# Content products of a lambda layer: four neighbouring blocks of q read innermost, PSUM written in strides

## The reference

```python
def lambda_layer(x, ...):                      # B=32, 128 channels, 64 x 64 pixels, 4 heads, DIM_K=16, 32 values
    q = bn(conv1x1(x, q_w), ...)
    k = conv1x1(x, k_w)
    v = bn(conv1x1(x, v_w), ...)
    pos = position_lambdas(emb, v)             # a 15 x 15 convolution of every value plane, 16 kernels
    k = jax.nn.softmax(k, axis=1)
    ...
    content_lambda = jnp.einsum('bkm,bvm->bkv', k, v2)
    content_out = jnp.einsum('bhkn,bkv->bhvn', q, content_lambda)
    position_out = jnp.einsum('bhkn,bkvn->bhvn', q, pos)
    out = content_out + position_out
...
residual = x                                   # x is the group-normalised input, 512 channels
h = jax.nn.relu(bn(conv1x1(x, conv1_w), ...))
h = lambda_layer(h, ...)
h = jax.nn.relu(bn(h, ...))
h = bn(conv1x1(h, conv3_w), ...)
out = input + jax.nn.relu(h + residual)
```

## Time and profile before

| | |
|---|---|
| time, median of 3 runs | 5148.84 us (5134.06 to 5149.53) |
| profiled execution, its time | 5146.99 us |
| profiled execution, its span | 5145.2 us |
| mean granted TensorE clock | 0.935 of full speed |
| TensorE busy | 4617.9 us (90%) |
| VectorE, ScalarE, GpSimd busy | 2959.7, 2286.6, 747.9 us |
| content products (L603), busy | 246.1 us |

### The profile page before, as it was taken

The page is one execution under the profiler, slowest core; times in us unless marked ns, Lnnn a source line. Parts: engine busy times, 40 slices in busy tenths (PEclk is TensorE's granted clock), DMA queues, the critical chain, the costliest instruction groups (busy, mean ns, idle before and its releaser), DMA issues.

```text
span 5145.2 us, 120758 instructions
## 1 busy us (share of the span) xinstructions
PE 4617.9 (90%) x49366; PEld 2712.5 (53%) x49366; DVE 2959.7 (58%) x4695; ACT 2286.6 (44%) x2816; POOL 747.9 (15%) x433
## 2 busy tenths in 40 slices
PE   4888999888999988999999999999989999999997
PEld 2555555554555554555555555555555555555554
DVE  4466565565555565655655556556556555566564
ACT  1444445444444444444444444444444444444443
POOL 0011111111110111111111101111011111111111
PEclk8899999999999999999889999999999999999998
DMA  3778767778777787777786777877777877778766
GB/s 95 222 251 292 256 223 262 249 260 294 239 232 257 252 283 261 223 257 248 259 290 216 247 250 255 293 252 225 257 259 263 289 220 243 255 255 295 257 219 231
DMA packets 537174, 1284.17 MB, mean 250 GB/s; under 512 B 43048, under 2 KB 225324, under 8 KB 528556
## 3 DMA queue, kind: packets, MB, share of 16 engines
q1 hardware_dynamic: 471276, 1017.22, 60.4%
q10 hardware_dynamic: 65472, 260.05, 13.7%
HBM read 844.79 MB, written 432.33 MB: 248 GB/s over the span
## 4 chain that ended last, share of the span: by engine, by line
PE 49%; issue 14%; DMA 12%; DVE 8%; SPq 7%; POOL 5%; ACT 4%; ACTq 0%; POOLq 0%; DVEq 0%
PE ring L523 16%; DMA X<-x_dram 10%; PE ring L649 10%; PE ring L504 9%; POOL X L1175 5%; PE ring L579 4%; PE ring L530 3%; PE ring L603 2%; DVE st L871 2%; PE ring L535 2%; SPq L400 2%; SPq L358 2%; PE ring L613 2%; DMA q_parts<-region 1%; ACT region L789 1%
## 5 line engine op out<-in xcount | busy, mean ns | idle before, releaser
L698 ACT COPY region<-ring 126x1024 f32<-126x1024 f32 x1184 | 1164.1, 1016 | 1101.3 <-PE ring L504 1092.0
L579 PE MATMUL ring<-h,w3T 128*128 128x512 f32 x2048 | 1009.6, 636 | 105.7 <-DVE S L1018 73.6
L504 PE MATMUL ring<-Qt,Ep 96*126 96x256 bf16 x5120 | 832.8, 302 | 177.1 <-DVE region L698 80.4
L523 PE MATMUL ring<-X,w1e 128*128 128x512 f32 x2048 | 908.0, 596 | 29.3 <-DVE w1e L895 29.3
L649 PE MATMUL ring<-region,V 126*32 126x128 f32 x24576 | 866.7, 285 | 26.6 <-issue 26.2
L504 PEld LDWEIGHTS ring<-Qt,Ep 96*126 96x126 bf16 x5120 | 605.2, 148 | 420.2 <-issue 167.8
L649 PEld LDWEIGHTS ring<-region,V 126*32 126x32 f32 x24576 | 668.6, 114 | 245.5 <-issue 237.6
L698 DVE COPY region<-ring 126x1024 f32<-126x1024 f32 x352 | 430.2, 1222 | 616.1 <-PE ring L504 616.1
L871 DVE BATCH_NORM_STATS2 st<-X 128x6 f32<-128x512 f32 x1024 | 624.5, 678 | 212.1 <-DMA X<-x_dram 212.1
L579 PEld LDWEIGHTS ring<-h,w3T 128*128 128x128 f32 x2048 | 387.7, 201 | 534.9 <-issue 388.4
L523 PEld LDWEIGHTS ring<-X,w1e 128*128 128x128 f32 x2048 | 385.0, 191 | 496.9 <-issue 493.6
(11 more groups left out here) (127 smaller groups left out, 2960.3 us busy)
## 6 DMA issues: line engine op xcount, KB each, us to landing
X<-x_dram SPq DMA_DIRECT2D x132, 2048.0 KB, 20.2
out_dram<-X SPq DMA_DIRECT2D x512, 512.0 KB, 9.6
X<-x_dram ACTq DMA_DIRECT2D x124, 2048.0 KB, 10.5
Qt<-q_parts SPq DMA_DIRECT2D x768, 128.0 KB, 2.8
V<-v_windows SPq DMA_DIRECT2D x96, 1024.0 KB, 9.4
lambda_sums<-S SPq DMA_DIRECT2D x64, 1024.0 KB, 4.1
h<-lambda_sums SPq DMA_DIRECT2D x256, 256.0 KB, 4.9
q_parts<-region SPq DMA_DIRECT2D x128, 256.0 KB, 3.3
```

What stands on the lines that cost most here:

```text
L504: last = nc.tensor.matmul(dst[0:TROWS, i * 256:(i + 1) * 256], taps(u, xo, yo), Q[:, :, xo * BLK + yo, :], start=(i % 2 == 0), stop=True, ...
L523: last = nc.tensor.matmul(dst[:, hh * HALF:(hh + 1) * HALF], w1e[:, c, :], X[:, j, c, hh * HALF:(hh + 1) * HALF], start=(c == 0), stop=(c ...
L579: last = nc.tensor.matmul(dst[:, yb * HALF:(yb + 1) * HALF], w3T[:, t, :], src, start=True, stop=True)
L698: return engine_copy(dst, src)
```

## The change

The content products read q in the order head, pixel, block, which is the order of memory, so that runs of four blocks come together. The PSUM operand is given the same order of indices: the block, which was the outermost of its three indices and lies 128 elements apart, is now the innermost. Each element of q goes to the PSUM element it went to before. Number, size and order of the instructions stay.

```diff
                     for c in range(NCH):
-                        nc.tensor.matmul(bank_of(k)[c * DV:(c + 1) * DV, :], CLp[:, :],
-                                         Qg[:, :, c, half * 32:half * 32 + 32, 4 * k:4 * k + 4]
-                                         .rearrange("p h n b -> p b h n"),
+                        nc.tensor.matmul(bank_of(k)[c * DV:(c + 1) * DV, :]
+                                         .rearrange("p (b h n) -> p h n b", b=4, h=HEADS), CLp[:, :],
+                                         Qg[:, :, c, half * 32:half * 32 + 32, 4 * k:4 * k + 4],
                                          start=True, stop=False, skip_group_check=True)
```

## The result

| | before | changed |
|---|---|---|
| median of 4 runs each | 5148.74 us (5134.06 to 5149.53) | 5093.17 us (5086.59 to 5105.84) |
| ratio, 95% interval | | 0.9904 (0.9887 to 0.992) |
| profiled execution | 5146.99 us | 5105.84 us |
| mean granted clock in it | 0.935 | 0.924 |

The kernel is 1.0% faster, 56 us. The profiled execution of the changed kernel is the longest of its four; its span is 41.1 us shorter than that of before, so what the traces add up to is 41 us and not 56.

What follows compares the result with a forecast made beforehand. TensorE, busy for 90% of the span, was taken to bound the kernel. Second call -85 us, first call 0, pauses +6: -79, so 5147 to 5068 us (5070 as median); range 5030 to 5152, the forecast's own 5055 to 5085.

Steps and rivals of the forecast that it cites:

- rival A: The content products' strided PSUM write runs at half pace, 0.85 ns per column: call 1.80 us, kernel 5094 us; chance 0.17.
- Where the calls lie: Two content calls per image: time saved in the first vanishes in the wait for VectorE; the second's saving counts fully.
- Read: Content's read of q: runs of four share a 32-byte step of 1.75 ns, 0.44 ns per column, call 1.00 us.
- Write: Content's PSUM write in 512-byte steps: no extra time taken, judged from L613, the only strided write in the trace.
- First call: Content for half 0, mostly at half clock: falls to 1.8 us, the wait grows by 1.85 us, net gain 0.
- late instructions: TensorE's unexplained pauses amid L649, read as instructions arriving late: 0.2 us more per image, 6 us in all.
- B: Content's strided write costs what the read did, or 8-byte runs don't cure the read: 5137 to 5149 us; chance 0.14.
- C: Content's PSUM write is dearer, from 1.75 ns per column upward; at 2.9 ns call 6.0 us, kernel 5234; chance 0.14.
- Rival D: Content call is short, but low clock and pauses behind the first call eat the gain: 5108 to 5127 us; chance 0.09.

Runs made afterwards that it cites:

- e6: Kernel before the change, with the new order of read and write in the first call (half 0) only: 5157.33 us, ratio 1.0006.
- e1: Changed kernel's read in runs of four, but PSUM written in one piece as before, in both calls (sums misplaced): 5094.52 us in one execution.
- e3: Both calls read 512 neighbouring elements of q and write PSUM in one piece (wrong values): 5076.62 us in one execution.
- e11: As e10, with the sixteen matmuls of the first call issued twice in the old order: 5133.3 us, ratio 0.9973 to the kernel before.
- e9: The changed kernel measured once more, new order in both calls: 5099.39 us, ratio 0.9899 to the kernel before.
- e10: Kernel before the change, with the new order in the second call (half 1) only: 5091.91 us, ratio 0.9886.
- e2: Changed kernel's PSUM write in 512-byte steps, but reading 512 neighbouring elements of q (wrong values): 5092.24 us in one execution.
- e12: Both calls read 512 neighbours and write every second PSUM element (8-byte steps), then those between (wrong values): 5123.54 us in one execution.
- e7: Both calls read 512 neighbours and write PSUM in pairs of neighbours, 512 bytes apart (wrong values): 5076.81 us in one execution.
- e8: Both calls read pairs of neighbours, 32 bytes apart, and write PSUM in one piece (wrong elements): 5108.76 us in one execution.
- e4: Kernel before the change, its old read kept but PSUM written in 512-byte steps (sums misplaced): 5148.39 us in one execution.

## Why the prediction held, point by point

The kernel is faster, as forecast, and its 5093 us lie within the range of 5030 to 5152. They do not lie within the forecast's own range of 5055 to 5085: what came true is rival A, which had 0.17 where the forecast had 0.42. The gain is 56 us instead of 79.

- *Where the calls lie* held in its outcome. From the second call to c0 the time fell by 2.14 us and the call itself by 1.97 (3.65 to 1.68). The first call is worth nothing: in e6 it gave back some 0.4 us per image and the kernel stayed as it was, and in e1, where it fell from 3.65 to 1.69 us, the stretch to the second call did not get shorter (37.38 against 36.81 us). The reason given holds only in part. "Whatever the first call gives back is added to that wait" is not what happened: in the changed kernel the wait for VectorE shrank, and in e1 it grew from 80.4 to 94.5 us, 14 us where the first calls had given back 2.0 x 32 = 63. The rest went with the clock, which was low for 13.4 us per image behind e1's first call and for 6.0 before the change.
- *Read* held: runs of four cure it (e1, 0.93 us against 1.00 forecast). The 16 fixed ns per quad do not show where four run at once: e3 needs 215 ns for 512 columns, 0.42 each.
- *Write* is the term that was mis-sized. I took no extra and had half pace as rival A; it is half pace, 0.83 ns per column, and the second call 1.68 us instead of 1.00. That is 0.68 x 32 = 22 us of the 23 us between 5070 and 5093, though other terms moved too, as the point on rival A says. The step that failed is how L613 was read. I split its 46 ns into a part that follows the clock and one that does not, and charged only the second with the write, as if the price of a step never followed the clock. That of the read does not; that of the write does. L649's price, 0.85 ns for a column of fp32 written in one piece, gives 16 columns 14 ns of the part that follows the clock; L613 has 24, nearly the 27 ns of half pace, so the sign of half pace stood in the earlier trace rows. The match is in numbers only; L613 was not tried with another write.
- *First call*: 1.8 us at half clock was forecast, 3.32 measured, for the same reason. Its waits were to grow from 80 to 140 us and fell to 64.4; TensorE's busy time was to fall by 140 us and fell by 33.4. The sum had put the first call at 0 in any case, so this mistake cost nothing there.
- *Rival A* said 5094 and its call 1.80 us; the kernel has 5093.17 and 1.68. By its own steps it would be 5147 - 1.97 x 32 = 5084, so 9 us came back elsewhere; I had put 6 down to late instructions. The pauses of L649 did not grow (26.2 to 25.5 us), and in e1 and e11 they went the other way than I had read them: 3.5 us with the shortest calls, 78.3 with the longest first call. So that cause falls, and that A's total comes out within 1 us is in part luck. The longer stretch behind the first call has the size (27 us in the profiled execution, the longest run; less in the others), and more of it lies at half clock; the medians of e9 and e10 do not decide whether the change does it.
- *Rivals B and C* fall with e1, e2 and e12: the write costs 0.83 ns per column at full clock, below the 1.75 at which C begins. By the rule of the Trainium skill, "PSUM — Partial Sum Buffer", Specifications (TRN2), writes that are not contiguous slow a matmul: the traces agree for single elements (0.86 to 1.68 us), and not for pairs of 8 bytes, though these are not contiguous either (e7, 0.85 us). By the Trainium skill, "SBUF — State Buffer", Door 1: The DMA port swizzle, two hits per line are enough: here two leave the call at 1.82 us, and four bring it to 0.93 (e8, e1; three were not tried).
- *Rival D* was right in that the clock takes back what the first call gives, and in nothing else: quads were not short, the waits of L504 for VectorE, which were to grow to over 4 us each, fell to 64.4 us in 58 waits with 3.0 as the longest, and the time from the second call to c0 did fall. e1, with short quads and 5094.52 us in its one execution, comes nearer to D; but there too the second call to c0 takes 23.69 us, and part of the low clock lies ahead of the wait already.

## What to carry to other kernels

Content took the same time at both levels of the clock, and the read of its moving operand set its pace. Where a matmul of another kernel does so too, look at the innermost step of that read and give it runs of four bf16 elements or more, even if PSUM is then written in single elements at half pace. Before a price from one row is carried to another, ask whether the price follows the clock, and ask it of each memory by itself. Then ask where the instruction lies: of two equal calls only the one without a wait and a low clock behind it gave back time.

## What I had not expected of the hardware

A PSUM write in single elements costs two TensorE cycles per column and so 0.83 ns at full and 1.67 ns at half clock, at steps of 8 bytes as of 512; in pairs of 8 bytes it costs nothing (0.85 us per call against 0.86 in one piece). A read of bf16 from SBUF in steps of 32 bytes costs 1.78 ns per step at either clock, and the elements of a run share it. Read and write prices overlap, the larger counts (e4, 3.66 us). All this is measured with bf16 operands and four matmuls at once on 32 partitions of PSUM each; one matmul alone, fp32, and reads at other steps were not tried.
